# One lane of a gather moved from GpSimd's indirect transfer to one-row transfers on SyncE

## What is computed

```python
ft = (feat @ W_fc).reshape(N, H, D)
e = leaky_relu(eh[src] + ee + et[dst], negative_slope=0.2)
ex = exp(e - segment_max(e, dst)[dst])
a = ex / segment_sum(ex, dst)[dst]
rst = segment_sum(ft[src] * a[:, :, None], dst) + bias
```

## Time and profile before

| | us |
|---|---|
| median of three runs | 5833.36 |
| span of the profiled execution | 5829.4 |
| GpSimd busy, all stages | 3454.1 |
| attention: first gather issued | 4324.6 |
| attention: last gather issued | 5368.8 |
| attention: last logits (L2207) | 5392.1 |
| last messages (L2284) | 5421.6 |

### The profile page before, as it was taken

How to read it: one execution, slowest core, us unless ns; L and a number is a source line. 1 busy time by engine, 2 the same in 40 slices (tenths; PEclk the granted TensorE clock), 3 DMA queues, 4 the chain that set the end, 5 groups by cost and what they waited for, 6 DMA issues and landing times. The chain is left out here.

```text
span 5829.4 us, 82423 instructions
## 1 busy us (share of the span) xinstructions
PE 4489.2 (77%) x21018; PEld 3259.2 (56%) x21019; DVE 2854.4 (49%) x7377; ACT 2011.1 (34%) x5278; POOL 3454.1 (59%) x3588
## 2 busy tenths in 40 slices
PE   3777777777777777777787649999967777777898
PEld 2555555544445444544444549999945555555566
DVE  5344444434434433333334533333358888888745
ACT  3444444433333333343334324444431111111221
POOL 2777777777777776777777352222227777776001
PEclk7888988877777776787777659999978888888899
DMA  7555555566666664554444452222245555554101
GB/s 212 137 140 138 139 139 139 137 196 188 191 197 188 188 196 123 163 157 141 139 138 141 141 174 36 36 36 36 35 153 170 165 170 167 165 166 141 57 1 44
DMA packets 484768, 790.56 MB, mean 136 GB/s; under 512 B 208029, under 2 KB 337814, under 8 KB 477622
## 3 DMA queue, kind: packets, MB, share of 16 engines
q0 software_dynamic: 179904, 468.85, 31.1%
q1 hardware_dynamic: 304502, 317.59, 16.8%
HBM read 591.79 MB, written 194.31 MB: 135 GB/s over the span
## 5 line engine op out<-in xcount | busy, mean ns | idle before, releaser
L981 POOL DMA_INDIRECT rows<-node_rows,psrc x2496 | 2360.9, 946 | 811.3 <-issue 393.6
L1247 PE MATMUL ps<-rows,hot 128*128 128x257 f32 x4992 | 1851.5, 497 | 737.2 <-DMA rows<-node_rows,psrc 582.4
L1062 DVE TENSOR_TENSOR shared<-shared,ps 128x257 f32 x2496 | 1055.8, 423 | 1775.8 <-PE ps L1247 1458.5
L1247 PEld LDWEIGHTS ps<-rows,hot 128*128 128x128 f32 x4992 | 1052.2, 240 | 1412.0 <-DMA rows<-node_rows,psrc 1061.2
L2183 POOL DMA_INDIRECT rows<-attn_table,psrc x832 | 792.1, 952 | 332.4 <-issue 234.6
L1179 ACT ACTIVATE hot<-iota_f,pdl 128x128 f32<-128x128 f32 x2496 | 758.5, 388 | 50.8 <-PE ps L1247 50.8
L2476 PE MATMUL ps<-rows,hot 128*128 128x264 f32 x1664 | 555.0, 482 | 197.2 <-DVE rows L2284 139.4
L1817 POOL DMA_INDIRECT resid<-feat,slot_node x105 | 165.0, 1571 | 622.9 <-DVE feat L1832 619.8
L2476 PEld LDWEIGHTS ps<-rows,hot 128*128 128x128 f32 x1664 | 353.9, 229 | 315.3 <-DVE rows L2284 149.8
L2305 DVE TENSOR_TENSOR sums<-sums,ps 128x264 f32 x832 | 356.6, 429 | 92.6 <-PE ps L2476 33.9
L1934 PEld LDWEIGHTS ps<-feat 128*128 128x128 f32 x3360 | 394.3, 193 | 8.4 <-DVE feat L1861 2.4
(11 more groups left out here) (458 smaller groups left out, 4462.9 us busy)
## 6 DMA issues: line engine op xcount, KB each, us to landing
slot_rows<-blank SPq DMA_DIRECT2D x112, 520.0 KB, 4.5
hot_table<-hot SPq DMA_DIRECT2D x104, 512.0 KB
hot<-hot_table SPq DMA_DIRECT2D x52, 1024.0 KB, 5.5
rows<-node_rows,psrc POOLq DMA_INDIRECT x2496, 2.8
feat<-in_edge_attr_dram SPq DMA_DIRECT2D x832, 32.0 KB
feat<-slot_rows SPq DMA_DIRECT2D x105, 130.0 KB
rows<-attn_table,psrc POOLq DMA_INDIRECT x832
node_rows<-shared SPq DMA_DIRECT2D x99, 128.5 KB, 3.9
```

The source lines that it names most:

```text
L981: g.indirect_dma_start(rows[:, n % RING, :], None, tables[k % 2], bass.IndirectOffsetOnAxis(ap=psrc[:, n:n + 1], axis=0)).then_inc(row_sem ...
L1062: v.tensor_tensor(row, row, ps[banks(k, i)[h * G + b]][:, 0:F + 1], ALU.add).then_inc(added.h, 1)
L1247: pe.matmul(ps[cycle[s]][:, 0:F + 1], hot[:, 2 * half + h, b, :], rows[:, slot, :], start=True, stop=True).then_inc(aggregated.h, 1)
```

## The change

In the gather of GpSimd, lanes 0 to 126 take part and lane 127 does not. For lane 127 SyncE reads eight entries of the last row of `psrc` into registers at a time, and issues a transfer of one row of `attn_table` for each pair. They stand in SyncE's queue between the edge terms and the starts of each group, in two halves of eight; from group 4 on, each half first waits on `summed` until the half of group n - 4 that used the buffer is summed up. VectorE's `all_terms` waits for a second semaphore, `last_lane_in`, beside `rows_in`.

```diff
@@ attend(), semaphores
             rows_in = [sem(f"rows_in{u}") for u in range(4)]
+            last_lane_in = [sem(f"attn_last_lane_in{u}") for u in range(4)]
@@ SyncE
                         if n >= 2:
                             sp.wait_ge(scanned.h, n - 1)
+                        for half in range(2):
+                            if n >= 4:
+                                sp.wait_ge(summed.h, 8 * (n - 4) + 4 * half + 4)
+                            sources = in_registers(sp, psrc[P - 1:P, bass.ds(n * AG + half * G, G)], N - 1)
+                            for b in range(G):
+                                sp.dma_start(rows[P - 1:P, u, half * G + b, :], attn_table[bass.ds(sources[b], 1), :]).then_inc(last_lane_in[u].h, 16)
                         sp.dma_start(starts[:, n % 2, :], start_table[n * P:(n + 1) * P, :]).then_inc(starts_in[n % 2].h, 16)
@@ GpSimd
-                        g.indirect_dma_start(rows[:, u, b, :], None, attn_table,
-                                             bass.IndirectOffsetOnAxis(ap=psrc[:, n:n + 1], axis=0)).then_inc(rows_in[u].h, 16)
+                        g.indirect_dma_start(rows[0:P - 1, u, b, :], None, attn_table,
+                                             bass.IndirectOffsetOnAxis(ap=psrc[0:P - 1, n:n + 1], axis=0)).then_inc(rows_in[u].h, 16)
@@ VectorE, all_terms
                             v.wait_ge(rows_in[u].h, 16 * AG * (turn + 1))
+                            v.wait_ge(last_lane_in[u].h, 16 * AG * (turn + 1))
```

## The result

The changed kernel takes 7986.42 us (median of 4 runs, 7982.74 to 7988.84) beside 5832.42 us before; the ratio is 1.3697, with a 95% interval of 1.3677 to 1.3716. That is +2154 us. The profiled executions differ by as much: 7986.9 - 5829.4 = 2157.5 us.

A forecast was written before the change was run, and what follows sets the result against it. GpSimd bounds the attention's start, then VectorE, TensorE and ScalarE set the turn. Uneven shares (0 to +1 us) and rotating engines (+7.3 to +9) gave +4 midway on the profiled 5829.4, 4.0 below the median: 5837 us; range 5826 to 9,400.

The forecast's parts named there:

- rival 1: GpSimd's issue of each attention gather becomes longer: prices from +479 to +5630 us; chance 0.42.
- What bounds the kernel, and the threshold: In the attention, gathers come each 1.257 us against 1.283 asked for; issue lengthened by under 0.026 us costs nothing after the start.
- 832 x d - 20.5: Price in us of longer attention gathers: d is the lengthening of each, 20.5 the lead used up.
- What it adds on SyncE: Sixteen one-row transfers and two register loads, 9.3 us in a turn with 18.3 free; cost 0, up to 1 us.
- Rival 3: SyncE becomes the bound in the attention: at 1.54 us a one-row transfer, +363, or 6196 us; chance 0.05.
- What it does to the gather: Open term for 127 rows on GpSimd's queue: uneven shares, 0 to +1 us, or one engine per gather, +7.3 to +9.
- the pace stays: Attention gathers stay at one in 1.257 us, with uneven shares or one engine per gather; chance 0.41, about half each.
- the quiet end: The choice that GpSimd's gather pace is unchanged, giving +4 us, 5837 us; chance 0.41.
- +1519: Price in us if GpSimd were held until each attention gather has landed, 2.8 us: 7353 us.
- The variant with one engine at a time: Each attention gather moves on one engine, successive ones on different engines; landing 7.3 us later, paid once; about half of 0.41.
- Rival 2: All attention gathers go to the same engine, 7.74 us each: +5374, or 11,200 us; chance 0.09.

The follow-up runs named there:

- e11: Changed kernel with GpSimd gathering 126 lanes from group 4 on, SyncE fetching lane 127's row from there, lane 126 left out: 5841.42 us, ratio 1.0015.
- e3: Kernel before with attention gathers of 126 lanes from pair 64 on, without SyncE's rows: 6657.18 us against 6657.66.
- e7: Kernel before with attention gathers of 124 lanes from pair 64 on, without SyncE's rows: 6715.48 us against 6675.62.
- e10: Kernel before with the 832 gathers of the third convolution on 127 lanes, lane 127 left out there: 7165.40 us against 5832.83.
- e9: Changed kernel with GpSimd gathering 126 lanes and SyncE fetching the rows of lanes 126 and 127, nothing left out: 5842.62 us, ratio 1.0018.

## Why the prediction was right, and where not

The time lies in the stated range, and the chance for slower was the largest (0.56). But the single forecast, 5837 us, was that of a case that did not come, and that 7986 lies in the range is in part luck: the range is that wide because the price of rival 1 was open by a factor of ten, and 847 of the 2154 us come from gaps that stand in no term of the sum.

- **What bounds the kernel, and the threshold.** Right. GpSimd's pace of 1.257 against VectorE's 1.283 us was the point on which all hung: +0.038 us in the instruction cost 8.6 us on chip C (e11), as the formula 832 x d - 20.5 has it with 768 gathers. On chips A and B the threshold is another, since the turn is longer there (in e3 GpSimd issues one gather in 1256 / 831 = 1.51 us): in e3 the same +0.038 cost nothing, and in e7 +0.336 cost 40 us.
- **What it adds on SyncE.** Right in substance. The sixteen transfers took 9.0 us in a turn (8.3 expected), the register loads 1.13 us each in the median where 0.53 was taken from the earlier trace rows, together 11.3 us for 9.3, of the 18.3 that were free. TensorE did not wait for `hot` after the start. Rival 3 did not happen.
- **What it does to the gather.** This is the step that failed. Of the two variants under "the pace stays" neither came. The second had the transfer right: the packets show a gather on one engine and the next on another, in 6.4 us where 7.7 was worked out. What it took for granted was that GpSimd's own instruction and its gap stay as they are; it went from 0.952 to 2.544 us, and long gaps of 1.020 us a gather came on top. The range of prices was open by a factor of ten, and the choice of the quiet end (0.41, beside 0.42 for rival 1) rested on nothing but that the instruction looked fixed at 0.946 us. The earlier trace rows had two gathers of the same 128 lanes; that they agree says nothing on other counts, as the text itself said.
- **Rival 1** is what happened (0.42). That the instruction goes by the rows of a share is shown by six counts of lanes: 0.946 us at 8 rows a share (128 = 16 x 8), 0.984 at 9 (126 = 14 x 9), 1.282 at 31 (124 = 4 x 31), 1.662 at 61, 2.353 at 113 and 2.54 at 127, the last three being primes: about 13.3 ns for each row of a share. The reason that the rival gave, sixteen lists made side by side, fits the short packets, which fill fifteen lists to the length of the sixteenth, but GpSimd's work itself is in no trace. Its price was mis-sized by a missing term. 832 x 1.592 - 20.5 = +1304 us follow from the instruction, and the long gaps, which no rival had, add 847. The nearest of the prices named, +1519, is right neither in its size nor in its parts; its idea, that GpSimd is held until a gather has landed, is near to what happens in the long gaps, but there it is paid once in seven or nine gathers.
- **The landing.** The variant with one engine at a time had 7.3 us more. Where each gather has a semaphore of its own (e10) it is 10.3 us for 2.8, so +7.5, of which 1.6 are the longer instruction.
- **Rival 2**, all gathers on one engine: 7.74 us a gather would have been the least pace by its reckoning, and 6.4 by the packets. The pace was 3.87, and 2.84 between long gaps, with the rows of two or three gathers under way at a time. It did not happen.
- The rule of the Trainium skill, "DMA: Bandwidth & Descriptors", section "Why a DMA increments its semaphore by 16 and not by 1", that the shares are the largest number up to 16 that divides the lanes, fits GpSimd's instruction and the packets at all six counts above, and its exception of uneven shares for some direct copies did not hold for this gather. That a share is one engine's work, so that 127 lanes run on one engine, this case's trace bears out as well, and of its turning of the engines at least that the next gather has another: one of 16 engines busy (6.2%) behind an issue that stood alone, and the rows of the next gather beside it. All packets of a gather together took 0.196 x 16 x 1000 / 259 = 12.1 engine-us (259 gathers between 5000 and 6000 us), but nearly half of that are the short ones.

## What to carry over

Before a partition is taken out of an indirect transfer that GpSimd issues, look at how the number of the remaining ones divides: on the issue 126 lanes cost 0.038 us and 124 a third, 113 and 127 make it two and a half times as long or more. A transfer's row in the profile with one shape tells little of another shape, and where an engine runs back to back with a margin of 2.8%, an unknown price on it should be taken as the likely case and not as the exception. One-row transfers on a queue with free time are cheap, 0.5 us each of the queue and nothing measurable of the end on chip C, but they bought nothing here: neither e9 nor e11 is faster than the kernel before, and none of the experiments points to a version that would be.

## What was not expected of the hardware

- GpSimd's indirect transfer costs about 13.3 ns for each row of a share and 0.84 us beside it. With fewer than sixteen shares but more than one it is some 0.025 us above that line (0.984 us at 9 rows where the line has 0.96, 1.282 at 31 for 1.25).
- Divided into sixteen shares a gather made 39926 / 832 = 48 packets; undivided it made 528, of which 32 carry the rows, four a packet, on one engine, and 480 are short ones, as many as fifteen further lists of the same length would make. All together took 12.1 engine-us for 7.7.
- The page's time to landing is not that of the rows where several gathers in flight share a semaphore: 7.9 us by the page, 9.6 us by the last packet with rows, and 10.3 by the page where each gather has its own (e10).
- With undivided gathers GpSimd stopped for mostly 8.0 or 8.8 us (127 lanes), 7.8 (113) and 5.5 (61), two, two and one time in sixteen gathers, each time until its queue was empty, and not at all in a convolution's gathers of the same 127 lanes. Why it stops there is open: a full buffer of about 1024 entries fits 8 and 16 gathers but not 7 and 9, and the two stages differ in how semaphores are shared and in more than that.
- The three chips differ by 14% in the kernel before (5833, 6658 and 6676 us), but by 0.2% in the stage that GpSimd alone sets (3213.1 and 3207.8 us).
